# Experts' routing moved sequence by sequence into the small attention ahead of it

## The reference

```python
def _L0_ffn_ref(...):
    x = x + _msa(_layernorm(x, ln1_w, ln1_b), w_qkv, w_proj)
    x = x + _moe_mlp(_layernorm(x, ln2_w, ln2_b), gate_w, gate_b, w1, w2)   # one expert a token: argmax of logits

def _L1_ffn_ref(...):
    x = x + _layernorm(_attention(x, ...), ln1_g, ln1_b)
    x = x + _layernorm(_moe(x, ...), ln2_g, ln2_b)     # the two best experts a token, by softmax(x @ gate_w + gate_b)
```

## Time and profile before

| | before |
|---|---|
| median of 3 runs | 4903.26 us (4899.63 to 4903.86) |
| the profiled execution's own time | 4894.49 us |
| its span, first to last instruction | 4892.8 us |
| granted TensorE clock, mean | 0.90 |
| busy: TensorE matmul, VectorE, ScalarE, GpSimd | 78%, 70%, 48%, 49% |
| instructions | 90894 |

### The profile page before, as it was taken

How to read it: one execution, slowest core, us unless ns; L and a number is a source line. 1 busy time by engine, 2 the same in 40 slices (tenths; PEclk the granted TensorE clock), 3 DMA queues, 4 the chain that set the end, 5 groups by cost and what they waited for, 6 DMA issues and landing times. The chain is left out here.

```text
span 4892.8 us, 90894 instructions
## 1 busy us (share of the span) xinstructions
PE 3823.4 (78%) x25840; PEld 2727.7 (56%) x25840; DVE 3405.3 (70%) x9524; ACT 2341.8 (48%) x5537; POOL 2392.6 (49%) x3948
## 2 busy tenths in 40 slices
PE   7889797779999799468868947568776887699475
PEld 5666565656666466366656636523332665466365
DVE  7888675556666677556658856669998664588566
ACT  3444464356666466234436634345553454266343
POOL 5666453434444443346644444367776663144443
PEclk9999898789999899689989968879988999899688
DMA  6000232100000133043323311211121331133113
GB/s 236 0 0 1 103 124 85 52 22 1 0 0 0 58 123 113 29 126 109 105 76 120 117 37 54 70 52 62 63 63 55 122 112 42 42 123 115 36 55 86
DMA packets 244547, 341.24 MB, mean 70 GB/s; under 512 B 26976, under 2 KB 187120, under 8 KB 243120
## 3 DMA queue, kind: packets, MB, share of 16 engines
q1 hardware_dynamic: 230960, 309.19, 19.0%
q0 software_dynamic: 13184, 27.22, 1.6%
HBM read 182.77 MB, written 147.26 MB: 67 GB/s over the span
## 5 line engine op out<-in xcount | busy, mean ns | idle before, releaser
L544 DVE TENSOR_REDUCE l0att_rowmax<-l0att_S 128x2 f32<-128x512 f32 x512 | 339.1, 686 | 130.6 <-PE l0att_S L724 128.5
L916 POOL TENSOR_TENSOR wb_prob<-wb_prob,wb_rden 128x128 f32<-128x128 f32 (+1 forms) x512 | 248.9, 508 | 360.7 <-DVE wb_rden L1093 360.2
L544 DVE TENSOR_REDUCE l1ffn_rowmax<-l1ffn_S 128x2 f32<-128x512 f32 x512 | 337.2, 686 | 90.9 <-PE l1ffn_S L724 83.5
L1990 POOL TENSOR_TENSOR ssm_hc<-core_AW_all,ssm_Cs 128x512 f32<-128x512 f32 x256 | 321.1, 1271 | 129.7 <-DVE core_AW_all L2136 96.6
L1455 POOL DMA_INDIRECT results<-e_y,e_back x220 | 210.6, 957 | 304.5 <-DVE e_y L1670 289.5
L958 ACT ACTIVATE wb_prob<-wb_biased,wb_nmax 128x128 f32<-128x128 f32 (+1 forms) x512 | 228.6, 447 | 236.9 <-DVE wb_nmax L1086 234.5
L2235 PE MATMUL ssm_Y<-ssm_hc,core_ident 128*128 128x512 f32 x512 | 288.6, 674 | 56.7 <-POOL ssm_hc L1990 30.5
L2136 DVE TENSOR_TENSOR_SCAN core_AW_all<-core_AW_all,ssm_U 128x512 f32<-128x512 f32 x256 | 310.3, 1212 | 1.1 <-ACT core_AW_all L2079 1.1
L724 PE MATMUL l1ffn_S<-l1ffn_K,l1ffn_Q 128*128 128x512 f32 x512 | 250.2, 492 | 76.9 <-DVE l1ffn_rowmax L544 44.7
L724 PE MATMUL l0att_S<-l0att_K,l0att_Q 128*128 128x512 f32 x512 | 246.8, 485 | 65.6 <-DMA l0att_K<-bounce 51.8
L2079 ACT ACTIVATE core_AW_all<-ssm_dt,ssm_A 128x510 f32<-128x510 f32 x256 | 178.5, 716 | 221.5 <-DVE core_AW_all L2136 219.8
(11 more groups left out here) (498 smaller groups left out, 11451.3 us busy)
## 6 DMA issues: line engine op xcount, KB each, us to landing
bounce<-l0att_parts SPq DMA_DIRECT2D x128, 256.0 KB, 2.8
bounce<-l1ffn_parts SPq DMA_DIRECT2D x128, 256.0 KB, 2.8
ssm_Cs<-c_rows SPq DMA_DIRECT2D x128, 256.0 KB, 3.0
routed<-core_Y SPq DMA_DIRECT2D x8, 2048.0 KB, 24.8
l0att_Q<-bounce SPq DMA_DIRECT2D x128, 128.0 KB
l0att_K<-bounce SPq DMA_DIRECT2D x128, 128.0 KB
bounce<-l1att_parts SPq DMA_DIRECT2D x64, 256.0 KB, 2.8
l1ffn_Q<-bounce SPq DMA_DIRECT2D x128, 128.0 KB
```

Of the source, the lines that this page charges most:

```text
L544: dve.tensor_reduce(out=rowmax[:, jp, qt, 2 * pair:2 * pair + 2], in_=S[a % 2][:].rearrange("p (j k) -> p j k", j=2)[:, :, 0:keys(qt)], op ...
L916: ins = pool.tensor_tensor(out=prob[:, w_ % NP, a:b], in0=prob[:, w_ % NP, a:b], in1=rden[:, w_ % NP, n:n + 1].to_broadcast([P, b - a]), o ...
L1990: pool.tensor_tensor(out=hc[:, u % 4], in0=hs[:, u % 4], in1=Cs[:, n % 4], op=ALU.mult)\
```

## The change

A new class `Router` holds the routing's buffers, and the attention ahead of the experts carries it out. The routing is by sequence for layer norm, transposes and logits, and by batch for the choice and the ranks: the batches are sequences 0-3, 4-7, 8-11, 12-13 and 14-15.

- In `small_attention` two pieces enter the plan, the transposes "yt" in slot 12 and the logits "lg" in slot 15, both for sequence r-2, and "rk", the ranks of a batch, in slot 14 (slot 8 in round 16). The rounds run to 18 instead of 16.
- VectorE: in l0 the statistics of the output right after `finish_out` (slot 13), and the normalisation in slot 10, in place in `core.Y`; the logits' bias in slot 15; `choose` and `locate` as generators of which two instructions are issued per slot (four in rounds 16 and later).
- A batch is chosen from slot 0 of the round 3 after its last sequence's (rounds 6, 10, 14, 16, 18).
- GpSimd: the power of -1/2 for l0, `carry_on` earlier in the round in l0, and the scatters: per round 1 + 1 in l0 and 3 + 1 in l1, the first ones between `normalise` and `part_max(r + 1, 0)`, the last one between `part_max` and `part`; from round 16 on all that wait, ahead of `out_power` and (l1) `carry_on`. What is left at the end goes in `experts`.
- Rows are scattered straight from `core.Yx`, which is `core.Y` with 8 more numbers a token: for each expert the destination in `results`. A row is 136 numbers instead of 130. In a turn VectorE picks the destination with the expert's register.
- The weights of l1 no longer travel with the row. `give` writes the bias sum straight to `y` (l0: a copy), and ScalarE multiplies the returned results with the weights before the join (`weigh`, 8 instructions a group).
- Small buffers are put together, and the clearing of `routed` takes 8 transfers of 136-number rows.

```diff
+class Router:
+    BATCHES = ((0, 4), (4, 8), (8, 12), (12, 14), (14, 16))
+    MOST = 4 * QT
+    FIRST_AT = 3
+    LATE = SEQS
...
+    def begins(self, r):
+        for b, (first, last) in enumerate(self.BATCHES):
+            if last - 1 + self.FIRST_AT == r:
+                return b
+        return None
+    def ranks(self, r, u):
+        b = self.begins(r)
+        return b if b is not None and u == (8 if r == self.LATE else 14) else None
...
+    def scatter(self, pool, core, most, batches):
+        while most and self.waiting and self.waiting[0][0] < batches:
+            b, t, k = self.waiting.pop(0)
+            pool.wait_ge(self.placed.sem, b + 1)
+            pool.indirect_dma_start(core.routed, bass.IndirectOffsetOnAxis(ap=self.pos_i[:, k, t:t + 1], axis=0),
+                                    core.Yx[:, t, :], None).then_inc(self.rows_sent.sem, 16)
+            most -= 1
...
+        if router:
+            plan.update({12: "yt", 15: "lg"})
...
+        ROUNDS = range(-3, SEQS + (3 if router else 1))
...
+            def scatters(r, most):
+                done = [b for b in range(len(router.BATCHES)) if router.BATCHES[b][1] - 1 + router.FIRST_AT < r]
+                router.scatter(pool, core, most if r < SEQS else len(router.waiting), len(done))
...
-            for r in range(-1, SEQS + 1):
+            for r in range(-1, ROUNDS.stop):
...
                 if inside(r + 3):
                     normalise(r + 3)
+                if router and router.normed_in and inside(r - 2):
+                    carry_on(r - 2)
+                    router.power(pool, core, r - 2)
+                if router:
+                    scatters(r, router.top + router.top // 2)
                 hide(r, 0, 8)
                 if inside(r + 1):
                     part_max(r + 1, 0)
+                if router and r < SEQS:
+                    scatters(r, 1)
                 if inside(r + 3):
                     part(r + 3)
                 hide(r, 8, 12)
                 last(r + 3)
                 if out_norm and inside(r - 1):
                     out_power(r - 1)
-                if carry and inside(r - 2):
+                if carry and not router.normed_in and inside(r - 2):
                     carry_on(r - 2)
...
                     elif x == "out":
                         finish_out(n)
+                        if router and router.normed_in:
+                            out_of(dve, "out", n)
+                            router.statistics(dve, routing, core, n)
...
+            def route(r, u):
+                b = router.begins(r)
+                if b is not None and u == 0:
+                    for n in range(*router.BATCHES[b]):
+                        out_of(dve, "lg", n)
+                    under_way.append(router.choose(dve, routing, core, b))
+                if router.ranks(r, u) is not None:
+                    assert not under_way
+                    out_of(dve, "rk", b)
+                    under_way.append(router.locate(dve, routing, core, b))
+                for _ in range(2 if r < SEQS else 4):
+                    if under_way and next(under_way[0], "ended") == "ended":
+                        under_way.pop()
...
             for j in range(NT):
                 pool.wait_ge(y_taken.sem, j + 1)
...
+            def weigh(g):
+                act.wait_ge(res_in[g % ENDS].sem, 16 * top * (g // ENDS + 1))
+                for k in range(top):
+                    for t in range(GT):
+                        x = res[:, k, g % ENDS, t]
+                        act.activation(x, x, ACT.Copy, scale=router.weight[:, k, g * GT + t:g * GT + t + 1])\
+                            .then_inc(weighted.sem, 1)
...
                 dve.wait_ge(y_made.sem, j + 1)
                 if b2 is not None:
-                    dve.tensor_tensor(out=biased[:, j % 2], in0=YB[j % 2][:, 0:D],
+                    dve.tensor_tensor(out=y[:, j % RING], in0=YB[j % 2][:, 0:D],
                                       in1=b2_all[:, bass.ds(expert[j], 1), :].rearrange("p o d -> p (o d)"),
-                                      op=ALU.add).then_inc(given.sem, 1)
-                    dve.wait_ge(given.sem, j + 1)
-                dve.tensor_scalar(y[:, j % RING], YB[j % 2][:, 0:D] if b2 is None else biased[:, j % 2],
-                                  got[:, j % RING, D + 1:D + 2], None, ALU.mult).then_inc(y_taken.sem, 1)
...
+                                      op=ALU.add).then_inc(y_taken.sem, 1)
+                else:
+                    dve.tensor_copy(y[:, j % RING], YB[j % 2][:, 0:D]).then_inc(y_taken.sem, 1)
...
+    for part in range(8):
+        sp.dma_start(whole[:, part * TILES * WIDTH:(part + 1) * TILES * WIDTH],
+                     core.Yx[:].rearrange("p t d -> p (t d)"))\
+            .then_inc(core.rows_cleared.sem, 16)
```

More of the change, by code:

```diff
@@ L23 @@
 EPS = 1e-5
+EXPERTS = 8
+WIDTH = D + EXPERTS
 MASKED = -1e30
@@ L505, in after_slot @@
                         act.activation(onT[:], F[:, 0:L], ACT.Copy).then_inc(gone(x, n), 1)
+                    elif x == "yt":
+                        given(n, x)
+                        await_(act, f_made, turn_of["lg", n - 1] + 1 if n else 0)
+                        if router.affine:
+                            act.activation(router.rT[:], F[:, 0:L], ACT.Identity, scale=router.affine[0],
+                                           bias=router.affine[1]).then_inc(gone(x, n), 1)
+                        else:
+                            act.activation(router.rT[:], F[:, 0:L], ACT.Copy).then_inc(gone(x, n), 1)
+                if router and router.top == 2 and u == 1 and router.begins(r) is not None:
+                    router.soften(act, router.begins(r))
                 for jp, at in ((1, 3), (0, 13)):
@@ L652, in _ @@
             dve.sem_inc(cleared.sem, 1)
-            for r in range(-1, SEQS + 1):
+            if router:
+                routing.step(dve.memset(router.before[:], 0.0))
+                dve.memset(router.before16[:], 0.0).then_inc(router.based.sem, 1)
+                routing.settle()
+            for r in range(-1, ROUNDS.stop):
                 for u in range(SLOTS):
@@ L661, in _ @@
                         finish_norm(r - 2)
-            if out_norm:
-                finish_norm(SEQS - 1)
+                    if router:
+                        if u == 10 and router.normed_in and inside(r - 2):
+                            dve.wait_ge(carried.sem, carried.at(r - 2))
+                            router.apply(dve, routing, core, r - 2)
+                        route(r, u)
+            for rest in under_way:
+                for _ in rest:
+                    pass
         @block.tensor
@@ L1367, in experts @@
             sig("back_ready"))
-        given = sig("given")
+        weighted = sig("weighted", GT * top)
         y_sent = [sig(f"y_sent{b}") for b in range(RING)]
@@ L1398, in _ @@
             sp.wait_ge(offsets_made.sem, 1)
-            for b in range(2):
-                sp.wait_ge(rows_sent[b].sem, SENDS * GROUPS // 2)
+            sp.wait_ge(router.rows_sent.sem, 16 * TILES * top)
             for j in range(NT):
@@ L1506, in _ @@
                     activate(j - 1)
+            if top == 2:
+                for g in range(GROUPS):
+                    weigh(g)
         @block.vector
@@ L1659, in give @@
                 await_(dve, y_sent[j % RING], 16 * (j // RING))
-                run(dve.tensor_tensor(out=back[:, j % RING, 0:1], in0=number(got[:, j % RING, D:D + 1]),
+                goes = got[:, j % RING, D:WIDTH].bitcast(U32)
+                run(dve.tensor_tensor(out=back[:, j % RING, 0:1], in0=goes[:, bass.ds(expert[j], 1)],
                                       in1=keep_i[:, j:j + 1].bitcast(U32), op=ALU.bitwise_and))
@@ L2634, in network @@
         l1_dense()
-        l1_ffn_attention(1)
-        l1_experts(1, out=out)
+        with ExitStack() as moe:
+            router = routing("l1", 1)
+            l1_ffn_attention(1, router)
+            l1_experts(1, router, out=out)
 def _program_inputs(inputs):
```

520 lines of the change are left out of this document (266 added, 254 removed).

## The result

The changed kernel takes **4698.0 us** (median of 4 runs, 4685.5 to 4703.7), the kernel before 4902.1 (4899.6 to 4903.9) on the same chip: ratio 0.958, 95% interval 0.9565 to 0.9599. The forecast was 4663, the range 4595 to 4740. The profiled execution has a span of 4697.2 us against 4892.8: 195.6 us less, where 240 were forecast. So the miss is 35 us by the medians and 44 by the profiles.

A forecast was written before the change was run, and what follows sets the result against it. No single engine bounds the kernel; the routing's serial chain is all on the path. Ends 125 + 143 and turns 45, less rounds 30 + 36, joins 5 and barriers 2, give 240 us: 4903.3 to 4663, range 4595 to 4740.

The forecast's parts named there:

- The ends, l0: Last l0 attention output to the experts' first turn: 83.7 us before, 21.2 after, 62.4 saved, twice 125.
- The ends, l1: End of l1 attention to first turn: GpSimd's 28 scatters set it, 71.5 us saved, twice 143.
- the barrier 1.2: In the l1 ends: 1.2 us for the barrier between GpSimd's attention work and the experts.
- The l1 turns: Turns of l1's experts: taking out `biased` with its wait saves 0.32 us in each of 142, 45 us.
- 1.97: Forecast length in us of an l1 experts turn, from 2.29 before, just above l0's turn.
- l0 rounds: Attention rounds in l0: added VectorE work costs 0.6 us x 15, plus 6 for batches; 15, twice 30.
- l1 rounds: Attention rounds in l1: 0.35 us x 12 ordinary, 4.5 x 3 of a batch; together 18, twice 36.
- A: Rival, chance 0.12: the rounds take the added work for nothing, only 7 us of costs stay, 4597.
- B: Rival, chance 0.14: l1 turns don't shorten, as the register read or TensorE takes the 0.32 us; 4708.
- C: Rival, chance 0.07: scatters and VectorE instructions block each other in the rounds, 108 x 0.2 us; 22 us, 4685.
- D: Rival, chance 0.12: added instructions land in full in the rounds, 204 us instead of 66; 4801.
- E: Rival, chance 0.04: slower; scatters ahead of `part_max` delay the maxima on top of D, rounds cost 340, 4937.

The follow-up runs named there:

- e7: Changed kernel, in round 16 the choice at two instructions a slot instead of four and the ranks in slot 14 instead of 8: 4692.3 us, ratio 0.958.
- e3: Changed kernel with the routing's normalisation in slot 8 of the l0 rounds instead of slot 10: 4677.2 us, ratio 0.955.
- e8: Changed kernel with eight scatters instead of four in l1's round 15, and l0 experts' loads ahead issued behind the first six fetches: 4685.8 us, ratio 0.9568.
- e5: Kernel before, with only l1's weights applied at the join by ScalarE and one VectorE instruction writing a turn's result: 4867.1 us, ratio 0.9932.
- e6: As e3, plus the statistics in slot 2 of the next l0 round instead of slot 13, except the last sequence's: 4659.6 us, ratio 0.9507.
- e1: Kernel before, with 39 more VectorE instructions ahead of wide attention b, so its loop begins at instruction 2422: 4919.7 us, ratio 1.0047.
- e2: Changed kernel with 89 more VectorE instructions ahead of wide attention b, so its loop begins at instruction 2511: 4679.2 us, ratio 0.9558.
- e4: Changed kernel with every scatter in the experts and none beside the rounds: 4879.8 us, ratio 0.996.
- e9: Changed kernel with e2's shift, e3's and e6's moves (sequence 14's statistics stay in slot 13) and e8's scatter move: 4639.2 us, ratio 0.9463.
- e10: As e9, but the choice at three instructions a slot in slots 2 to 10, places in slots 2 to 4 of the next round: 4646.5 us, ratio 0.9485.

## Why the prediction was right in kind, and what it mis-sized

- **The ends, l0** (61.8 us a stage forecast to be saved behind output 14, 57.9 and 62.2 measured). The chain of the last batch on VectorE runs as worked out: the last places are there 9.5 us behind the last output, forecast 10.7 (the last step of that sum, 841.4 + 4.1, is 845.5 and not 845.7). Two things were not in it. The last output comes 9.6 us behind the one before it, and not 8.1: with the choice and ranks of round 16 moved it is 8.4 and 8.9 (e7), but with the normalisation moved alone it is 8.4 too (e3), so it isn't theirs alone. And in the first stage SP issues the loads for wide attention b just ahead of the last scatters: the first fetch stands 6.9 us behind the last scatter, 3.3 in the second stage, and the first turn 24.3 us behind the last output, 20.4 in the second stage and 21.4 in e8 with those loads moved. I had counted only what the step itself issues.
- **The ends, l1** (71.5 us a stage forecast, 65.4 and 66.2 measured). Right: GpSimd sets them, by 28 scatters at 1.26 us, and `out_power` stands behind 12 (L639 at 2808.59). The step "the barrier 1.2" failed: it is 5.7 us from the last addition's end to the experts' first instruction, as GpSimd's drain takes 4.6 with scatters ahead of it. I had taken the barrier from the end of an attention without scatters; the experts' ends in the same trace, with drains of 7.3 and 7.6 us, were the rows to read. Of the 6 us missed, another 1.1 are three scatters in the experts that take 1.56 to 1.72 us in place of 1.26.
- **The l1 turns** (0.32 us a turn forecast, 0.24 measured; e5 alone gives the same). The circle was the right one; "1.97" failed, as about every second turn has the long copy of the weights, and the short ones stop at TensorE's 1.90.
- **l0 rounds** (0.6 forecast for an ordinary one, 1.3 measured). The statistics cost what was said: with the normalisation out of GpSimd's way (e3) 0.7 are left, and they go with the statistics (e6). The step "the normalisation, 0.6, falls in a gap of 0.7 in slot 10 or 11" failed: it takes 1.61 beside L620. The wait for K (8.6 us) is gone, as forecast; in its place TensorE waits 18.8 us for the maxima. The rounds of a batch cost less than said: 0.6 us on top of an ordinary one (19.5 against 18.9), forecast 2.
- **l1 rounds** (36 forecast, 26 measured). 0.1 to 0.3 for an ordinary round and 3.8 for the two rounds that a batch touches (21.1 + 19.1 against 18.2 twice), forecast 0.35 and 4.5 + 0.35: more of it was hidden by VectorE's waits than I took. In the 14 rounds VectorE has 18.4 us more work and waits 4.9 us less for TensorE's scores (26.3 before, 21.4 after). That all rounds together come to 62 us, where 65 were forecast, is luck: l0 is 7 above and l1 10 below. The sign given for "right", rounds of 18.2 and 18.9 us on the mean, reads 18.5 to 18.7 in both.
- **Joins** (5 forecast, 4.6 measured), right.
- **What the sum had no term for:** 16.4 us in wide attention b (e1, e2), some 11 of instruction fetch and 5 of the clock behind it. The other way, GpSimd's drain at the end of the l0 experts takes 5.0 us and not 7.3, which makes each 2.3 us shorter; in e4 it is 7.3 again, and why isn't shown. Wide attention b is the largest single part of the 44 us between forecast and profile. The others: 11 each in the turns and in l1's ends, 7 in l0's rounds, 4 in its ends, 5 in all other stages, and 10 the other way in l1's rounds.
- **Rivals.** A fell, as the rounds took 62 us; B fell (e5), C (e4), and D and E by the rounds' length. The sign was safe since the ends alone gave 252 us, and the costs on the other side came to 90.

**Still open.** TensorE's granted clock falls from 1.00 to 0.50 (of the two levels, 2.4 and 1.2 GHz) for some 3 us at a time, 48 times in the 14 rounds of the 36 l0 and l1ffn attentions of the 9 traces with the routing in them (e6 has one), and once in the 12 of the three without it (before, e1, e5). The attention l1att, which has no experts behind it, has 9 to 13 such falls in every trace, the kernel before's too. One round with a fall and the same round of the other l1 attention without, in the windows view of the changed kernel:

```profile
2622.85:2643.74 20.89, 18.79 (x156) 13.54 (x155) 17.47 (x48) 11.05 (x22) 12.35 (x21) 0.92 0.30 102
4275.47:4294.59 19.12, 17.52 (x156) 13.02 (x155) 17.31 (x48) 11.14 (x22) 12.40 (x21) 1.00 0.33 112
```

It costs 1.8 us there. TensorE had waited for the maxima for 0.76 us, and the clock fell within the next such wait, of 1.04 us. Other rounds have such waits and no fall. In wide attention b the falls come behind waits of 2.1 to 2.4 us, and there too not every time (3 of 5 turns of the changed kernel, 4 of 5 of e1). So waits of TensorE go ahead of the falls, but what decides isn't shown; five of them, at 1.4 to 1.9 us, are 8 us of the changed kernel's 62. Open as well is the wait for K in e9's and e10's second l0 attention.

## What to carry to other kernels

When a serial chain is moved beside a loop of work, its place there matters as much as its length: of 1.3 us in an ordinary l0 round, all could be saved by two moves of some slots, one into a wait that the timeline showed and one away from a GpSimd instruction that shut it out. Ask of every moved step what it now stands ahead of: a drain at the end of the block, loads on SP's queue, the next instruction of GpSimd's. The price of such a thing may stand in the trace before, at another stage's end. And look at the stages that the change doesn't touch: a loop repeated without instruction fetches at one place in the code may need them at another, and 39 instructions ahead of it cost 16 us here, a third of it through the clock that falls once TensorE is kept waiting.

## What the runs showed of the hardware that I had not expected

- A loop of 364 VectorE instructions ran without instruction fetch when it began at instruction 2383 or 2511 (turns of 78.5 us, five traces), and with five packets of 8 KB a turn at 2422 (seven traces): VectorE then stands still for 2.5 to 2.8 us behind the branch, and a turn takes 80.6 to 80.9 us, or 82.2 to 82.5 where the granted clock falls to 0.50 behind that wait (26 of 35 turns).
- GpSimd's drain takes 4.6 to 8.0 us when scatters stand ahead of it in its block, in all twelve traces (0.03 to 0.7 at the end of small attentions without them). At the end of the changed kernel's first l1ffn attention it ends 5.5 us after the last scatter's packets had moved.
- A VectorE tensor_scalar of 0.34 us takes 1.36 beside a GpSimd subtraction of 1.29 us. A copy of 0.43 us takes up to 0.67 beside a scatter of 0.96, but only when it starts 0.50 to 0.73 us behind the scatter's start (63 of 63 long ones in the changed kernel); 0.50 us or less behind it, 139 keep their 0.43.
